# Adapter routing and two gated FFNs on one core: a scaled weight copy cut in four for VectorE, gathers, waits and products set in another order

## The reference, cut to what matters

```python
# stage 0
z = einsum('bct,bcd->bdt', x, weights[itok])          # per-sample 32 x 32 mix
logits = z @ Wg + bg                                   # top 2 of 4 experts, softmax over the two
for i in range(4):                                     # the 1024 best scores of expert i
    sel_p, sel_idx = top_k(score_i, 1024)
    out[sel_idx] += gelu(z[sel_idx] @ W1[i]) @ W2[i] * sel_p
x = x + out
# stage 1: adapters of rank 16 on all three products
h = silu(lora(x, Wg, Ag, Bg)) * lora(x, Wu, Au, Bu)
y = lora(h, Wd, Ad, Bd)
x = x + y @ (weight * scale_weight[:, None]).T + bias
```

## Time and profile before

| | |
|---|---|
| time, median of 3 runs | 587.57 us (587.41 to 590.31) |
| the profiled execution's own time | 588.83 us |
| its span | 587.0 us, 10367 instructions |
| PE busy | 562.7 us (96%), 3583 matmuls |
| DVE busy | 372.0 us (63%) |
| ACT busy | 242.4 us (41%) |
| POOL busy | 142.6 us (24%) |
| chain that ended last | PE 89%, DVE 5%, DMA 3%, POOL 1%, issue 1% |

### The profile page before, as it was taken

The page is one execution under the profiler, slowest core; times in us unless marked ns, Lnnn a source line. Parts: engine busy times, 40 slices in busy tenths (PEclk is TensorE's granted clock), DMA queues, the critical chain, the costliest instruction groups (busy, mean ns, idle before and its releaser), DMA issues.

```text
span 587.0 us, 10367 instructions
## 1 busy us (share of the span) xinstructions
PE 562.7 (96%) x3583; PEld 470.0 (80%) x3583; DVE 372.0 (63%) x901; ACT 242.4 (41%) x545; POOL 142.6 (24%) x122
## 2 busy tenths in 40 slices
PE   4778999999999999999999999999999999999996
PEld 3556899999999999978878878788788788787885
DVE  7989668656776567665574575575665645754733
ACT  2645558747766655653322322324124123123110
POOL 3001402657446442664012030030030030100000
PEclk9999999999999999999999999999999999999999
DMA  8994666884285231732004022041041040120012
GB/s 327 340 358 164 205 237 187 228 186 68 53 229 169 46 46 17 201 54 73 0 10 135 10 93 59 3 129 25 0 135 17 0 141 11 64 59 5 12 26 36
DMA packets 64798, 61.04 MB, mean 104 GB/s; under 512 B 37456, under 2 KB 56656, under 8 KB 63472
## 3 DMA queue, kind: packets, MB, share of 16 engines
q1 hardware_dynamic: 53312, 37.97, 21.3%
q0 software_dynamic: 9264, 22.22, 15.5%
q10 hardware_dynamic: 2176, 0.26, 0.3%
HBM read 45.17 MB, written 19.47 MB: 110 GB/s over the span
## 4 chain that ended last, share of the span: by engine, by line
PE 89%; DVE 5%; DMA 3%; POOL 1%; issue 1%; SPq 0%; ACT 0%; DVEq 0%; POOLq 0%
PE bank L1429 25%; PE bank L1431 24%; PE bank L1430 24%; PE bank L1698 5%; PE bank L1656 3%; DMA xT<-in_xT 1%; DMA x_first<-x_rows,x_row 1%; PE bank L1536 1%; DMA xg<-flat_rows,slot_row 1%; PE bank L1545 1%; PE bank L1648 1%; PE bank L1445 1%; PE bank L1665 1%; PE bank L1666 1%; PE bank L1786 1%
## 5 line engine op out<-in xcount | busy, mean ns | idle before, releaser
L760 ACT ACTIVATE act<-bank 128x512 f32<-128x512 f32 x64 | 38.2, 598 | 183.0 <-PE bank L1698 183.0
L1385 DVE TENSOR_TENSOR prod<-bank,act 128x512 f32<-128x512 f32 x64 | 44.2, 690 | 97.7 <-PE bank L1698 97.3
L1241 DVE TENSOR_TENSOR hid_lo<-hf,hid_hi 128x512 fp32r<-128x512 f32 (+1 forms) x80 | 46.6, 585 | 52.9 <-ACT hf L681 52.4
L1429 PE MATMUL bank<-w_hi,hid_hi 128*128 128x256 f32 x256 | 71.8, 280 | 0.0
L1430 PE MATMUL bank<-w_lo,hid_hi 128*128 128x256 f32 x256 | 71.4, 279 | 0.0
L1431 PE MATMUL bank<-w_hi,hid_lo 128*128 128x256 f32 x256 | 71.3, 279 | 0.0
L678 ACT ACTIVATE hid_hi<-bank 128x512 fp32r<-128x512 f32 (+1 forms) x80 | 41.1, 514 | 64.8 <-PE bank L1431 63.3
L507 POOL DMA_INDIRECT x_rows<-y_sb,slot_row x32 | 52.1, 1628 | 42.5 <-ACT y_sb L648 24.6
L531 POOL DMA_INDIRECT b_pair<-b_rows,b_row x8 | 8.2, 1028 | 200.7 <-PE bank L1746 200.0
L1429 PE MATMUL bank<-xs_hi,w_hi 128*128 128x512 f32 (+1 forms) x158 | 56.5, 357 | 0.0
L1431 PE MATMUL bank<-xs_hi,w_lo 128*128 128x512 f32 (+1 forms) x158 | 55.0, 348 | 0.0
(11 more groups left out here) (323 smaller groups left out, 1258.6 us busy)
## 6 DMA issues: line engine op xcount, KB each, us to landing
w_raw<-in_L_ffn_W SPq DMA_DIRECT2D x8, 1024.0 KB, 6.9
flat_rows<-x_sb SPq DMA_DIRECT2D x8, 520.0 KB, 5.3
x_sb<-in_x SPq DMA_DIRECT2D x8, 512.0 KB, 8.7
x_rows<-in_x SPq DMA_DIRECT2D x4, 1024.0 KB, 8.6
outT<-out_sb SPq DMA_DIRECT2D x120, 32.0 KB, 1.6
xT<-in_xT SPq DMA_DIRECT2D x3, 1024.0 KB, 7.4
xT<-in_xT SPq DMA_DIRECT2D x2, 512.0 KB, 10.6
wdT<-in_wdT SPq DMA_DIRECT2D x1, 1024.0 KB, 6.0
```

The costliest lines, as they stand in the source:

```text
L760: act.activation(act1[h % 2][:, :], bank[h % 2][:, :], ACT.Silu).then_inc(silu1, 1)
L1241: dve.tensor_tensor(lo[:, n], hf[s % 2][:, n], hi[:, n].bitcast(f32), ALU.subtract).then_inc(hid0, 1)
L1385: dve.tensor_tensor(prod[par][h][:, :], bank[2 + h % 2][:, :], act1[h % 2][:, :], ALU.mult).then_inc(prod1, 1)
L1429: pe.matmul(out, lh, rh, start=start, stop=False, skip_group_check=True)
```

## The change

The scaled copy `wfT_s` is made by DVE instead of POOL, as four pieces of 128 x 128, one behind the questions of each of search steps 6 to 9; DVE waits for the fold weights in step 5; PE waits for four pieces. The candidates for step 5 are made ahead of `low_keys`. Step 4 has four rows of `item`, steps 8 and 9 have one. `gather(0)` waits for the stores (`flat_out`, `spare_out`) after its wait for `route_out`, no longer ahead of it. PE does item 36 ahead of `first_transposed(0)` and its filler products between the first two transposes; ACT evicts item 36 ahead of `first_hi(0)`. The third and fourth transposes follow steps 1 and 3. POOL issues `gather_b(1)` behind `gather_bd(0)`. `from_last` is cut by rows: its first part stands ahead of the last down product, and the first row of k = 1 ahead of the rest of k = 0.

```diff
-        ROW_STEPS = [2] * SEARCH_STEPS
+        ROW_STEPS = [2, 2, 2, 2, 4, 2, 2, 2, 1, 1]
...
+        LATE_STEPS = (1, 3)
@@ gpsimd
                 pool.wait_ge(route_out, e + 1)
+                if b == 0:
+                    pool.wait_ge(flat_out, 128)
+                    pool.wait_ge(spare_out, 32)
...
-            pool.wait_ge(mixed, 4)
-            pool.wait_ge(fold_w_in, 48)
-            pool.tensor_tensor(wfT_s[:, :, :], wfT[:, :, :], wf_scale.unsqueeze(1).to_broadcast([P, KD, D]),
-                               ALU.mult).then_inc(fold_in, 1)
-            pool.wait_ge(flat_out, 128)
-            pool.wait_ge(spare_out, 32)
             gather(0)
...
             pool.wait_ge(packed_in, 1)
-            for t in range(2):
-                gather_b(t)
+            gather_b(0)
...
             gather_x1(1)
-            for t in range(2):
-                gather_bd(t)
+            gather_bd(0)
+            gather_b(1)
+            gather_bd(1)
@@ scalar
-            first_hi(0)
             act.wait_ge(item_mm, ITEMS)
             act.activation(raw_bd[:, 0, :], bank[(ITEMS - 1) % 4][:, 0:D], ACT.Copy).then_inc(item_ev, 1)
+            first_hi(0)
             first_hi(1)
...
-                if s in (1, 2):
-                    first_hi(s + 1)
-                if s == 2:
+                if s in LATE_STEPS:
+                    first_hi(2 + LATE_STEPS.index(s))
+                if s == LATE_STEPS[1]:
                     slot_scales(0)
@@ vector
-                    done(dve.tensor_scalar(key[hf_][:, :, :], key_f[hf_][:, 1, :, :], 0.0, 2.0 ** LOW_BITS - 1, ALU.max, ALU.min))
+                    last_ = done(dve.tensor_scalar(key[hf_][:, :, :], key_f[hf_][:, 1, :, :], 0.0, 2.0 ** LOW_BITS - 1, ALU.max, ALU.min))
+                return last_ - 1, last_
...
                 if i == HIGH_STEPS:
+                    dve.wait_ge(fold_w_in, 48)
                     done(dve.tensor_scalar(thr_high[:, :], kept[0][HIGH_STEPS % 2][:, :, CAND], 2.0 ** LOW_BITS, None, ALU.mult))
+                if i > HIGH_STEPS:
+                    n = (i - HIGH_STEPS - 1) * P
+                    r = (slice(None), n // D, slice(n % D, n % D + P))
+                    dve.tensor_tensor(wfT_s[r], wfT[r], wf_scale[:, r[2]], ALU.mult).then_inc(fold_in, 1)
...
                 if i + 1 == HIGH_STEPS:
+                    next_cand(i + 1, 0, first)
                     second = best(i, 1, second)
-                    low_keys((first, second))
-                    first = next_cand(i + 1, 0, first)
-                    second = next_cand(i + 1, 1, second)
+                    next_cand(i + 1, 1, first)
+                    first, second = low_keys((first, second))
...
-                if s in (1, 2):
-                    first_lo(s + 1)
+                if s in LATE_STEPS:
+                    first_lo(2 + LATE_STEPS.index(s))
@@ tensor
-                    pe.wait_ge(fold_in, 1)
+                    pe.wait_ge(fold_in, 4)
...
+            item(ITEMS - 1)
             first_transposed(0)
-            item(ITEMS - 1)
+            pe.wait_ge(item_ev, ITEMS - 1)
+            keep_busy(WAIT_ROWS, bank[2], w1)
             first_transposed(1)
             pe.wait_ge(item_ev, ITEMS)
-            keep_busy(WAIT_ROWS, bank[2], w1)
             pe.wait_ge(lo0, LO_W1)
...
-                if s in (1, 2):
-                    first_transposed(s + 1)
+                if s in LATE_STEPS:
+                    first_transposed(2 + LATE_STEPS.index(s))
...
+            def from_last(k, rows):
+                for q in rows:
+                    for j in range(2):
+                        q_, j_ = (q, j) if q < 2 else (2 + j, q - 2)
+                        if k == 0:
+                            pe.wait_ge(y_lo if j_ else y_hi, q_ + 1)
+                        elif q == 0 and j == 0:
+                            pe.wait_ge(y_lo, 2)
+                        last = pe.matmul(bank[4 + k][:, :], y_last[j_][:, q_, k * P:(k + 1) * P], pick[:, q_, :],
+                                         start=q == 0 and j == 0, stop=q == GB - 1 and j == 1, skip_group_check=True)
+                if rows[-1] == GB - 1:
+                    last.then_inc(pick_mm, 1)
+
+            pe.wait_ge(pick_in, GB)
+            pe.wait_ge(y_lo, 1)
+            from_last(0, range(2))
             down(STEPS0 - 1, split=True)
...
-            pe.wait_ge(pick_in, GB)
-            for k in range(KD):
-                from_last(k)
+            from_last(1, range(1))
+            from_last(0, range(2, GB))
+            from_last(1, range(1, GB))
```

More of the change, by code:

```diff
@@ L1777, in _ @@
             pe.wait_ge(lo1, len(SPLITS1))
-            def from_last(k):
-                pe.wait_ge(y_lo, k + 1)
-                for q in range(GB):
-                    for j in range(2):
-                        q_, j_ = (q, j) if q < 2 else (2 + j, q - 2)
-                        if k == 0:
-                            pe.wait_ge(y_lo if j_ else y_hi, q_ + 1)
-                        last = pe.matmul(bank[4 + k][:, :], y_last[j_][:, q_, k * P:(k + 1) * P], pick[:, q_, :],
-                                         start=q == 0 and j == 0, stop=q == GB - 1 and j == 1, skip_group_check=True)
-                last.then_inc(pick_mm, 1)
-            pe.wait_ge(pick_in, GB)
-            for k in range(KD):
-                from_last(k)
+            from_last(1, range(1))
+            from_last(0, range(2, GB))
+            from_last(1, range(1, GB))
             def first_hi(k, h, sides=(0, 1)):
```

## The result

The changed kernel takes 587.28 us in the median of 22 runs, the kernel before 588.25 in as many beside it: a ratio of 0.9977, with a 95% interval of 0.9968 to 0.9987, which is -1.35 us (-0.76 to -1.88). The profiled execution of the changed kernel took 587.32 us, with a span of 585.5 us against 587.0.

The account below looks back on a forecast made before the run. PE was taken to bound the kernel after a front of some 62 us. Front 2.12 us (1.75 + 0.37) plus passage 1.15 gave 3.27 off 587.57, so 584.3 us; range 583.6 to 586.0.

Parts of the forecast that it names:

- the passage: Between the two kinds of experts: later `gather_b(1)` and PE's new order bring the low rank's start 1.15 us earlier.
- The step between the keys: Search, high to low keys: without POOL's copy and with candidates ahead, questions come 1.15 us earlier; bounds 0.2 and 1.2.
- The pieces: Four copy pieces on DVE behind search questions: 0 cost each, at most 0.11 each, 0.44 in all.
- the fold weights' wait: DVE's new wait in search step 5, at about 38.4: costs 0, with 1.0 us to spare.
- the rows of `item`: Fewer rows in the last search steps, where PE waits for DVE: cost 0, gathers' waits for stores no later.
- The first gather's wait: Tile 0's gather after `slot_row`: tile 2's order of waits starts it 0.60 us sooner; bounds 0 and 0.60.
- The order at the first tile: First expert tile: item 36 fills PE's 1.05 us wait; later fourth transposes no longer meet their gather, gaining 0.37 us.
- the fourth transposes' 0.37: First expert tile: moved from step 2 to step 3, the fourth transposes no longer wait for their gather, 0.37 us.
- The pause: PE before x_first's transposes: 1.39 us lost; 2.9 us less DMA traffic ahead removes it; bounds nothing or all 1.39.
- the first ("the passage keeps its pause"): Rival, 15%: x_first may still land late at the passage; 1.15 us lost, giving 585.5 us.
- The third (slow issues beside VectorE's splits): Rival, 8%: DVE's work blocks the first gathers' issues on GpSimd; 0.87 us lost, giving 585.2 us.
- the fifth: Rival, 7%: `gather(1)` or loads behind it become late in the first expert tile; 586 to 587.4 us.

Follow-up runs that it names:

- e1: The kernel before, unedited, run against itself: ratio 0.9988, two identical kernels 0.7 us apart.
- e3: The kernel before with only the passage's changes, the gathers' order and PE's order together: +0.6 us, ratio 1.001.
- e5: The kernel before with only PE's new order at the passage: +0.2 us, ratio 1.0003.
- e8: The kernel before with GpSimd's scaled copy waiting until the sixth search step's questions are out: -0.7 us, ratio 0.9988.
- e13: The kernel before, unedited, against itself again in the second comparison: ratio 1.0.
- e7: The changed kernel without its passage part, against the kernel before: -1.6 us, ratio 0.9973.
- e14: The changed kernel, unedited, a fourth time against the kernel before: -2.0 us, ratio 0.9966.
- e15: The changed kernel with PE's old order at the passage, second run, against the kernel before: -2.65 us, ratio 0.9955.
- e16: The kernel before with the search's part and the place of the gather's two waits, second run: -2.2 us, ratio 0.9963.
- e2: The kernel before with the search's part alone (copy in four pieces on VectorE, item rows, order between the keys): -1.2 us, ratio 0.9979.
- e11: The kernel before with the search's part and the place of the gather's two waits, first run: -2.2 us, ratio 0.9962.
- e12: The changed kernel without its passage part, second run, against the kernel before: -1.7 us, ratio 0.9971.
- e4: The changed kernel, unedited, run again against the kernel before: -0.35 us, ratio 0.9994.
- e9: The changed kernel with PE's old order at the passage, gathers' new order kept, against the kernel before: -1.8 us, ratio 0.9969.
- e10: The changed kernel, unedited, on one chip with three variants, against the kernel before: -0.5 us, ratio 0.9991.
- e6: The kernel before with only the first tile's start changed (gather's waits, last item, transposes): -0.6 us, ratio 0.999.
- third group: Four runs on chip 8 against the kernel before, e9 to e12: -1.8, -0.5, -2.2 and -1.7 us.
- second and fourth: Groups e5 to e8 on chip 5 (ratios 1.0003, 0.999, 0.9973, 0.9988) and e13 to e16 on chip 1 (1.0, 0.9966, 0.9955, 0.9963), against the kernel before.

## Why the prediction was wrong

The forecast was 3.27 us, and the four comparisons of the changed kernel gave 1.35, 0.35, 0.5 and 2.0, 1.06 in the mean. The step that failed is the passage.

**The step between the keys** held: 1.15 forecast, 1.16 to 1.20 by all eleven profiles with it, against the three of the kernel before; 0.12 of it is the order of the candidates (2.71 to 2.59), the rest the copy. Its mechanism, GpSimd's copy in VectorE's way, is shown by the stall that moves with the copy (e1, e3, e5, e8). That the copy's overlap fell on L896 was chance; into the search's chain it fell in all seven profiles that have it.

**The pieces, the fold weights' wait, the rows of `item`** cost nothing, as forecast.

**The first gather's wait** held for the gather: 0.60 forecast, 0.59 measured, in every kernel that has it. PE got 0.45 of it, since VectorE's second `xs_lo` ended last. I had the two sides ending together; my 60.29 for that `xs_lo` is 0.08 short of its own terms (59.61 + 0.34 + 0.42), and it ended 6.32 behind `slot_row` where I had 6.23.

**The order at the first tile** gave nothing that lasts. From `slot_row` to the point at which PE could begin the transposes of x_first (the last product before them plus 0.12), the profiles of the old start in which ScalarE was nowhere late have 193.84 (before), 193.46, 193.44 and 193.56 us (e5, e8, e13); those of the new start 192.93 to 192.96 (after, e7, e14, e15), and e16, with the wait's place alone, 192.99. So 0.5 us is gained, and 0.9 against the first profile, where I had 0.60 + 0.37: the fourth transposes' 0.37 was one execution's.

**The passage** was forecast at 1.15 and costs instead. Two terms of it failed.
- The pause. I took the 1.39 us of the one profile for a property of the kernel. In the eleven profiles with the old order of gathers the pause is 1.24, 0.96, 0.45, 0.26, 0.16 and six times nothing: 0.28 in the mean. It goes with the group of runs: on chips 0 and 8 it is nothing in all four (e1, e2, e11, e12), and every pause is in the other seven, the first profile (of a chip that the record doesn't name) and those on chips 5 and 1, 0.44 in the mean. The price of the 1 MB ahead of x_first was mis-sized with it. I had 2.9 us of delay. From the last issue of x_first to the start of GpSimd's next scatter, which waits for it, it is 3.6 to 4.0 us on chips 0 and 8 and 4.8 to 6.2 in the others with the 1 MB ahead, and 3.3 and 4.7 to 5.0 without: the 1 MB costs 0.45 and 0.5 us in the mean.
- The price of the new order. My own chain of it came to 5.37 us from the transposes on (249.05 to 254.42); the old order takes 5.11 without a pause. So the sum held a loss of 0.26 that I never named, since I set it against the end of the old order with its pause in. It measured 0.57 more than 5.11, 5.68; of the 0.31 beyond my chain, 0.19 had come by VectorE's addition, 4.18 behind the start of the transposes where I had 3.99. The mechanism was in the working: the last down product releases the second half of `y_last`, which ScalarE, VectorE, PE and VectorE pass on in turn. With four selections put ahead, that product comes 0.9 later; the selections of k = 1 put in their place fill only a part of what PE then has to wait.

With these two the account closes for three of the four comparisons, by estimates from the stretches. Search and start give 1.18 + 0.5 = 1.7; the passage adds a loss of 0.57 less the pause that the old order would have had. For the first comparison and chip 1, with 0.44 of pause, that is 1.6, against 1.35 and 2.0 measured. On chip 0 there is no pause to save, and in e4 ScalarE was late (below), so that `slot_row` to the passage took 194.5 us there against 194.0 to 194.2 in e1, e2 and e3: 1.18 - 0.4 - 0.6 = 0.2, against 0.35. On chip 8, where the kernel before was not profiled, it stays open: the changed kernel gained 0.5, but e9, e11 and e12, with the same late ScalarE, 1.7 to 2.2. The six comparisons of kernels with the search's part and the wait's place, and without PE's new order, gave 1.6 to 2.65, 2.0 in the mean. The direct differences of the two orders of PE are 0.65 (e15 against e14) and 1.3 (e9 against e10) by the ratios, 0.14 and 0.5 by the medians; it is the stretch, 5.66 to 5.68 us in six profiles and 5.06 to 5.11 in twelve, that tells them apart.

Of the rivals, the first ("the passage keeps its pause") was nearest in its place, but not in its mechanism: the pause was mostly not there to be kept. The third (slow issues beside VectorE's splits) showed once, in e6. The others didn't show, though something did become late in the first expert tile, as in the fifth: ScalarE, and neither `gather(1)` nor a load. (The fifth's times should read 585.7 to 587.3, by its own 1.4 to 3.)

The changed kernel with PE's old order at the passage (e9, e15) gave -1.8 and -2.65 us. The search's part with the gather's wait alone does as well (-2.2, -2.2), with far less of an edit, and the stretches say the same: 192.99 against 192.95 us to the passage.

**What stays open.** xT was waited for until 7.1 or 7.2 us in all seven profiles of kernels with the copy on GpSimd, and until 7.0 to 8.5 in the eleven with the search's part, five of them over 7.5. Whether the change does this, through the placing of its program or otherwise, or chance does, wasn't tried. ScalarE's pause of 2.7 to 2.8 us came in e4 and in all four kernels of the third group, and in none of the second and fourth, where four of the same kernels ran. So it goes with the chip, or with the time at which its group ran, as the pause before x_first does in the other direction: all five are from chips 0 and 8. All five also have the search's part and the gather's new wait; near that place e1, e2 and e3, on chip 0, have a pause of 1.3 to 1.4 us. In the five it costs 0.9 us or more from one `slot_row` to the next (31.6 to 31.7 against 30.7). No releaser in the trace explains it.

## What to carry to other kernels

A pause in one profile is a sample. Before a pause behind a DMA is booked as a gain, a second profile of the unchanged kernel, on another chip, should show it again; a stall that hangs on two engines' instructions meeting did come back every time here, with another instruction's name on it. And where an edit fills a pause by taking work out of order, price the new order once with the pause and once without it: here it gained 0.6 us in the one case and lost 0.6 in the other.

## What the runs showed of the hardware

**VectorE and GpSimd.** While GpSimd's copy ran (1.26 to 1.28 us in five profiles), the VectorE instruction with its inputs in SBUF that started beside it lasted until its end: L896, L874 of 1.32, L892 of 1.43, L862 of 1.05, all of 0.15 to 0.36 otherwise. Compares that were under way were not slowed in e5 (0.69), and the copy took 1.51; in e13 a compare that started 0.14 us into the copy took 1.45. A reduction out of PSUM ran through at 0.22. The Trainium skill (SBUF — State Buffer, the section on the two sides) has this as a port pair that the two engines lock for whole instructions, not as a shared bandwidth; the traces agree, in both directions. What I had not expected is that so narrow an instruction as one of 4 elements a partition pays the whole 1.25.

**TensorE's clock.** Nine of the eighteen profiles have a stretch in the front at a granted clock of 0.5, that is 1.2 GHz. e1's windows, before and in it:

```profile
36.00:40.00 4.00, 1.85 (x29) 1.36 (x26) 3.81 (x19) 0.77 (x2) 1.28 (x1) 1.00 1.03 409
40.00:44.00 4.00, 3.97 (x28) 2.69 (x28) 3.21 (x19) 1.26 (x4) 0.00 (x0) 0.57 1.05 374
```

PE had been busy for 1.85 of 4 us ahead of it, with its wait for the keys in that time; but the first profile of the kernel before has 1.86 of 4 there and kept the full clock, so this alone doesn't decide. Two of e1's search steps then took 2.17 and 2.41 us in place of 1.95, 0.68 in all; where the low clock fell just before the search, as in e4, the search started 1.0 to 2.0 us later. Much of the scatter of some 3 us between runs of one kernel goes with this. The record has the mean granted clock of every run: 0.990 to 0.996 in the nine profiled executions with such a stretch, 0.998 or more in the nine without. Over the 321 runs of the four groups, those under 0.998 are 1.6 us longer, chip and kernel held equal (a fit, so an estimate). 10 of the changed kernel's 35 runs are at 0.998 or more, and 28 of 160 of the kernel before. At an equal level the changed kernel gains 0.8 us by that fit, and the three kinds of kernel without PE's new order (e7 and e12, e9 and e15, e11 and e16) 1.5 to 1.65.
